# Rope by halves and probabilities split before their turn, in a four-layer kernel on one core

## The chip, the core and the metric

The kernel runs on one core of a Trainium2 chip. The metric is the device time of one execution in microseconds (us). The engines are TensorE (PE, with its weight loads PEld), VectorE (DVE), ScalarE (ACT), GpSimd (POOL) and SyncE (SP), which issues most of the transfers. Each runs its own list of instructions in the order in which the kernel writes them, and they wait for each other by semaphores.

## The reference, cut to what matters

Two layers, each of attention and a feed-forward part, over 16 batches of 128 tokens with 512 features. The change is in the first attention (and a little in the expert part behind it):

```python
x = x + xattn(layernorm(x), ctx)           # <- the change is in here
x = x + moe(layernorm(x))                  # 16 experts, 6 per token; its last blocks change order
x = x + memory_attention(layernorm(x), ctx)
x = x + peer_and_mlp(layernorm(x))

# xattn, 16 heads, per batch of 128 queries and 128 keys
kv_c, q_c = kv @ W_kvc, q @ W_dq
q_nope, q_rope = q_c @ W_uq, rope(q_c @ W_qr)      # rope on 64 columns per head
k_nope, v, k_rope = kv_c @ W_uk, kv_c @ W_uv, rope(kv_c @ W_kr)
scores = (q_nope . k_nope + q_rope . k_rope) * scale, masked by seg_id
out = softmax(scores) @ v @ W_o
# rope: concat(x1*cos - x2*sin, x1*sin + x2*cos)
```

The weights W_uk and W_uv are folded into the query and output weights ahead of this stage. Products are made of 16-bit pairs: a value is held as `hi` (rounded to 16 bits) and `lo` (what is left), and `mm3` issues three matmuls, hi by hi, hi by lo, lo by hi.

## The kernel before

The attention stage is a software pipeline of 64 **steps** (`STEPS`). Step m works on tile t = m // 4 (a batch of 128 tokens) and on head group g = m % 4 (four heads). In one step TensorE does, in this order: the scores of step m; the query product of the next tile's group (`heads_pe`) and, for g 0 and 1, the next tile's rope product in halves of eight heads (`rope_pe`); the turn of the probabilities of step m-2 (`turn_prob`); the value product of step m-3; the output product of step m-4. So each product's operands are made by the other engines in the steps between.

**The probabilities.** `exps(m)` on ScalarE writes exp(scores) into `prob`, in float32. VectorE takes the reciprocal of the sums at the start of its next step (`reciprocals`, L1560). GpSimd multiplies (`normalize`, L2092, in place). In step m+2 TensorE turns four 128x128 float32 squares into bank 2 (L887), ScalarE copies them as `pt_hi` (`prob_high`, L1250), VectorE writes `pt_lo` from the bank and `pt_hi` (`prob_low`, one `lo_of`, L1461), and `values` takes both in step m+3.

**The rope.** For the next tile, VectorE multiplies by cosine and sine in steps g=0 and g=1 (`rope_dve`, L1540, L1544). In step g=2 GpSimd adds the two products over all 16 heads (`rope_sum_pool`, L2084), ScalarE rounds the sum to 16 bits (`rope_act`, L1220) and GpSimd writes the rest (`rope_low_pool`, L2088). TensorE turns the first eight heads late in step g=3 (`rope_turn(t + 1, 0)`, L846), ScalarE copies them out right behind `exps` (`rope_copy`, L1224), and the scores of the next tile's first step (L871) wait for that copy.

**What else lies in these queues.** For finished tiles there is a chain of one tile in four steps: `row_rstd` (g=0); `row_normalize` on VectorE, `row_high` on ScalarE (L1261) behind `exps`, `row_low` on GpSimd (L2102), all g=1 from step 9; a turn and its copy `rows_turned` (g=2, L1277); `logits` (g=3). GpSimd issues batches of four scatters of token numbers (`place_batch`, L2106) at the end of three steps in eight from step 19. Two pieces of expert weights per step, in steps 0 to 55, are split into halves by ScalarE (`split_act`, L1289) and VectorE (`split_dve`, L1461 on SBUF operands). ScalarE's order in a step is: `heads_act` (L1231), `prob_high`, `values_high`, `exps` (L1237 and L1242), `row_high`, `rows_turned`, `rope_act`, `rope_copy`, `split_act`. VectorE's is: `reciprocals`, `maxima`, a split, `heads_dve`, `prob_low`, `values_low`, `rope_dve`, routing, a split.

The expert stage behind it runs 111 blocks (`NBLK`) through `expert_up`, `turn_rows`, `turn_hidden` and `expert_down`; each block's output goes out by an indirect add to `x_sum` (L2175), one after the other.

## Time and profile before

| what | us |
|---|---|
| median of 3 runs | 2100.8 |
| lowest and highest | 2089.52, 2101.47 |
| profiled execution, its own time | 2079.02 |
| its span, first to last instruction | 2077.2 |
| attention stage, first scores to the end of the routing | about 180 to 712 |
| expert stage | about 732 to 1450 |
| memory attention, then the last feed-forward part | to 2077 |

The profiled execution was faster than all three timed runs, so sums are made against 2079.0 and carried to the median as a difference. TensorE is busy 88% of the span, VectorE 59%, ScalarE 42% and GpSimd 39%. In a row of the timeline the first number is the start in us from the span's start, the second the duration; a bracket at the end says how long the engine stood idle before and what released it. "L2084" is a line of the kernel before; most lines name one operation, but L1461 is the helper `lo_of` and L205 to L207 are `mm3`.

### The profile page before, as it was taken

Reading aid. Unit: us, or ns where it says so; the run is one execution under the profiler, and the core shown is the slowest. Engines: PE = TensorE matmul, PEld = TensorE weight load, DVE = VectorE, ACT = ScalarE, POOL = GpSimd, SP = SyncE. Lnnn points to the kernel's source line nnn. Section 1 sums busy time; section 2 is a strip of 40 time slices with the busy share of each in tenths; the row PEclk is TensorE's granted clock in tenths of the full one; section 3 lists DMA queues with packets and bytes.
Section 4 is the critical chain, followed back from the end, with each engine's and each line's share of the span. In section 5 each row is a group of like instructions: output and inputs, shape, how many; then the busy total and the mean of one; then the engine's idle time right before and its main releaser. Section 6 shows DMA issues by size and latency. Waiting matters only on the chain.

```text
span 2077.2 us, 39689 instructions
## 1 busy us (share of the span) xinstructions
PE 1834.4 (88%) x13029; PEld 1085.9 (52%) x13029; DVE 1225.5 (59%) x2650; ACT 875.3 (42%) x1774; POOL 809.9 (39%) x659
## 2 busy tenths in 40 slices
PE   2575999989889389999999999996569989999998
PEld 1334666656656156666666666664434434444443
DVE  7854787877776333343333333331785677777776
ACT  3435777777776134344444444442232222212211
POOL 3102336554565533443344334432101334544542
PEclk6697999999999789999999999998789999999999
DMA  5313558667675266666666665544200346565554
GB/s 196 111 61 106 174 172 176 186 160 186 155 173 133 55 176 167 143 148 169 141 158 144 149 167 113 97 90 69 97 35 4 114 143 199 166 209 198 192 183 162
DMA packets 149136, 294.82 MB, mean 142 GB/s; under 512 B 40432, under 2 KB 77936, under 8 KB 144688
## 3 DMA queue, kind: packets, MB, share of 16 engines
q1 hardware_dynamic: 97968, 157.48, 26.4%
q0 software_dynamic: 46368, 126.29, 24.8%
q10 hardware_dynamic: 4608, 8.52, 1.3%
q8 instruction: 116, 1.90, 0.4%
q14 instruction: 76, 0.62, 0.1%
HBM read 426.00 MB, written 78.33 MB: 243 GB/s over the span
## 4 chain that ended last, share of the span: by engine, by line
PE 68%; DVE 10%; issue 6%; POOL 6%; ACT 5%; DMA 4%; SPq 0%; POOLq 0%; ACTq 0%; DVEq 0%
PE bank L205 19%; PE bank L206 19%; PE bank L207 19%; POOL expert_tokens L2106 3%; PE bank L999 2%; DVE work_arena L1461 2%; PE bank L1026 2%; DVE work_arena L168 1%; DVE ln_st L155 1%; ACT xt_arena L1242 1%; POOL work_arena L2088 1%; DMA work_arena<-in_moe_w 1%; POOL xt_arena L2092 1%; DMA work_arena<-in_ctxT 1%; DMA x_sum<-x,work_arena 1%
## 5 line engine op out<-in xcount | busy, mean ns | idle before, releaser
L205 PE MATMUL bank<-work_arena,xt_arena 128*128 (+1 forms) x1285 | 417.1, 327 | 0.9 <-ACT xt_arena L1370 0.9
L206 PE MATMUL bank<-work_arena,xt_arena 128*128 (+1 forms) x1285 | 416.9, 326 | 0.0
L207 PE MATMUL bank<-work_arena,xt_arena 128*128 (+1 forms) x1285 | 416.8, 326 | 0.0
L2175 POOL DMA_INDIRECT x_sum<-x,work_arena x111 | 175.5, 1581 | 400.0 <-ACT x L1389 201.9
L205 PE MATMUL bank<-work_arena 128*128 128x512 f16 (+1 forms) x680 | 261.8, 387 | 47.6 <-DVE work_arena L1461 18.8
L1934 DVE TENSOR_TENSOR xt_arena<-xt_arena,bank 128x352 f32<-128x352 f32 x111 | 57.8, 521 | 371.2 <-PE bank L207 371.2
L206 PE MATMUL bank<-work_arena 128*128 128x512 f16 (+1 forms) x680 | 261.7, 387 | 0.0
L207 PE MATMUL bank<-work_arena 128*128 128x512 f16 (+1 forms) x680 | 260.1, 384 | 0.0
L205 PE MATMUL bank<-xt_arena,work_arena 128*128 128x512 f16 (+1 forms) x560 | 212.7, 380 | 1.0 <-DVE xt_arena L174 1.0
L206 PE MATMUL bank<-xt_arena,work_arena 128*128 128x512 f16 (+1 forms) x560 | 212.5, 379 | 0.0
L207 PE MATMUL bank<-xt_arena,work_arena 128*128 128x512 f16 (+1 forms) x560 | 212.4, 379 | 0.0
L1370 ACT ACTIVATE xt_arena<-bank 128x1024 f16<-128x1024 f16 x111 | 113.7, 1024 | 222.1 <-PE bank L999 222.1
L2182 POOL TENSOR_TENSOR work_arena<-work_arena 128x512 f16<-128x512 f32 x64 | 73.6, 1170 | 270.5 <-ACT work_arena L1355 270.5
L1461 DVE SCALAR_TENSOR_TENSOR work_arena<-work_arena 128x1024 f16<-128x1024 f32 (+3 forms) x117 | 140.7, 1203 | 63.6 <-ACT work_arena L1289 55.7
L207 PEld LDWEIGHTS bank<-work_arena,xt_arena 128*128 128x128 f16 x1285 | 126.5, 98 | 85.3
L205 PEld LDWEIGHTS bank<-work_arena,xt_arena 128*128 128x128 f16 x1285 | 126.5, 98 | 80.6 <-issue 1.0
L206 PEld LDWEIGHTS bank<-work_arena,xt_arena 128*128 128x128 f16 x1285 | 126.5, 98 | 80.1 <-issue 0.3
L2191 POOL DMA_INDIRECT work_arena<-in_pk_e,work_arena x128 | 136.2, 1064 | 35.0 <-issue 31.3
L205 PEld LDWEIGHTS bank<-work_arena 128*128 128x128 f16 x680 | 69.7, 102 | 126.2 <-DVE work_arena L1461 24.5
L1461 DVE SCALAR_TENSOR_TENSOR work_arena<-bank,work_arena 128x512 f16<-128x512 f32 (+1 forms) x176 | 110.4, 659 | 31.6 <-ACT work_arena L1250 9.8
L2162 POOL DMA_INDIRECT x<-token_rows,work_arena x111 | 110.4, 995 | 44.4 <-issue 26.5
L1757 DVE SCALAR_TENSOR_TENSOR x<-bank,x 128x512 f32<-128x512 f32 x128 | 88.2, 691 | 60.3 <-PE bank L207 60.2
(255 smaller groups left out, 3793.4 us busy)
## 6 DMA issues: line engine op xcount, KB each, us to landing
work_arena<-expert_w SPq DMA_DIRECT2D x111, 1408.0 KB
work_arena<-expert_w SPq DMA_DIRECT2D x111, 768.0 KB
work_arena<-in_moe_w SPq DMA_DIRECT2D x64, 352.0 KB
expert_w<-work_arena SPq DMA_DIRECT2D x86, 176.0 KB
work_arena<-in_moe_w SPq DMA_DIRECT2D x48, 256.0 KB
work_arena<-in_mlp_w SPq DMA_DIRECT2D x8, 1536.0 KB, 9.6
work_arena<-in_head_w SPq DMA_DIRECT2D x16, 512.0 KB, 3.6
expert_w<-work_arena SPq DMA_DIRECT2D x64, 128.0 KB
```

Of the source, the lines that this page charges most:

```text
L205: pe.matmul(o, a_hi, b_hi, start=start, stop=False)
L206: pe.matmul(o, a_hi, b_lo, start=False, stop=False)
L207: return pe.matmul(o, a_lo, b_hi, start=False, stop=stop)
L1370: act.activation(xT[:, b % 2, :], bank[4][:, :].bitcast(F16), ACT.Copy).then_inc(xt_cp, 1)
L1461: return dve.scalar_tensor_tensor(out=o, in0=src, scalar=scale, in1=hi, op0=ALU.mult, op1=ALU.subtract)
L1757: dve.scalar_tensor_tensor(out=xv, in0=bank[6 + q % 2][:, :], scalar=1 / (WS * WS), in1=xv, op0=ALU.mult, op1=ALU.add).then_inc(xadd[q % 2 ...
L1934: dve.tensor_tensor(em[:, b % 2, :], esg[:, b % 2, :], bank[2 + b % 2][:, 0:MOE_D], ALU.mult).then_inc(e_m, 1)
L2106: pool.indirect_dma_start(out=recs[:, :], out_offset=bass.IndirectOffsetOnAxis(ap=ridx[:, t, k:k + 1], axis=0), in_=rtok[:, t:t + 1].bitca ...
L2162: pool.indirect_dma_start(out=xbu[:, b % XB, :], out_offset=None, in_=rows[:, :], in_offset=bass.IndirectOffsetOnAxis(ap=rid[:, i:i + 1], ...
L2175: pool.indirect_dma_start(out=xacc[:, :], out_offset=bass.IndirectOffsetOnAxis(ap=rid[:, i:i + 1], axis=0), in_=ysb[:, b % YB, :], in_offs ...
L2182: pool.tensor_tensor(h_lo[:, S_ % 2, c, :], m2[:, c, :], h_hi[:, S_ % 2, c, :], ALU.subtract).then_inc(hlo, 1)
L2191: pool.indirect_dma_start(out=gbuf[:, n % 2 * SETS + i - FIRST[n], :], out_offset=None, in_=ins["pk_e"][:, :], in_offset=bass.IndirectOffs ...
```

## The change

Three things are done.

1. **Rope by halves.** `rope_sum_pool`, `rope_act` and `rope_low_pool` work on eight heads at a time (a = 0, 1), twice as many instructions of half the size. The first half's sum and rounding move to step g=1, its rest to g=2; the second half follows one step behind. `rope_turn(t + 1, 0)` moves ahead in step g=3, to right behind the query product.
2. **Probabilities split first.** `normalize` writes its product as 16 bits into a new buffer `prob16`. `prob_low` now reads SBUF alone (`prob` in float32 and `prob16`), in four instructions of 128x128 that scale by the reciprocal, and runs one step earlier (m-1 in place of m-2), behind GpSimd's `normalize` of the same step. `turn_prob` turns eight 16-bit squares. `prob_copy` takes them out in one copy of 128x1024, in place of `prob_high` and the old `prob_low`. `prob` has two buffers in place of three. The factor 64 on the probabilities is gone.
3. **The last expert blocks** are put in another order on TensorE, so that each turn of the hidden values stands behind an `expert_down`.

The gate weights' buffers move to another place in memory.

```diff
             def turn_prob(m):
-                pe.wait_ge(normed, m + 1)
-                need(pe, ptl, m)
-                for i in range(4):
-                    last = pe.transpose(bank[2][:, i * P:(i + 1) * P], prob[:, m % 3, i, :], id32[:, :])
+                pe.wait_ge(plow, m + 1)
+                need(pe, pt_cp, m)
+                o = bank[2][:, :].bitcast(F16)
+                for i in range(8):
+                    last = pe.transpose(o[:, i * P:(i + 1) * P], prob16[:, m % 2, i * P:(i + 1) * P], id16[:, :])
                 last.then_inc(pt_mm, 1)
...
                     if g < 2:
                         rope_pe(t + 1, g)
+                    if g == 3:
+                        rope_turn(t + 1, 0)
...
-                if g == 3 and t + 1 < NT:
-                    rope_turn(t + 1, 0)
...
-            for b in range(NBLK):
-                if b + 1 < NBLK:
-                    expert_up(b + 1, slots[b + 1])
-                if b + 2 < NBLK:
-                    slots[b + 2] = slot_of(b + 2)
-                    turn_rows(b + 2)
+            for b in range(NBLK - 2):
+                expert_up(b + 1, slots[b + 1])
+                slots[b + 2] = slot_of(b + 2)
+                turn_rows(b + 2)
                 turn_hidden(b)
                 if b > 0:
                     expert_down(b - 1, slots.pop(b - 1))
-            expert_down(NBLK - 1, slots.pop(NBLK - 1))
+            expert_down(NBLK - 3, slots[NBLK - 3])
+            turn_hidden(NBLK - 2)
+            expert_up(NBLK - 1, slots[NBLK - 1])
+            expert_down(NBLK - 2, slots[NBLK - 2])
+            turn_hidden(NBLK - 1)
+            expert_down(NBLK - 1, slots[NBLK - 1])
...
-            def rope_act(t):
-                act.wait_ge(rope_sum, t + 1)
+            def rope_act(t, a):
+                hs = slice(8 * a, 8 * a + 8)
+                act.wait_ge(rope_sum, 2 * t + a + 1)
                 if t > 0:
-                    act.wait_ge(tr_mm, tr_at["turn", t - 1, 1] + 1)
-                act.activation(rhl[:, :, 0, :], rot, ACT.Copy).then_inc(rope_h, 1)
+                    act.wait_ge(tr_mm, tr_at["turn", t - 1, a] + 1)
+                act.activation(rhl[:, hs, 0, :], rot[:, hs, :], ACT.Copy).then_inc(rope_h, 1)
...
-            def prob_high(m):
+            def prob_copy(m):
                 act.wait_ge(pt_mm, m + 1)
                 need(act, o_mm, m - 1)
-                act.activation(pt_hi[:, m % 2, :], bank[2][:, :], ACT.Copy, scale=PS).then_inc(pth, 1)
+                act.activation(pt[:, m % 2, :], bank[2][:, :].bitcast(F16), ACT.Copy).then_inc(pt_cp, 1)
...
                 if t + 1 < NT:
-                    if g == 2:
-                        rope_act(t + 1)
+                    if g in (1, 2):
+                        rope_act(t + 1, g - 1)
...
             def prob_low(m):
-                dve.wait_ge(pth, m + 1)
-                lo_of(pt_lo[:, m % 2, :], bank[2][:, :], PS, pt_hi[:, m % 2, :]).then_inc(ptl, 1)
+                dve.wait_ge(normed, m + 1)
+                for i in range(4):
+                    last = dve.scalar_tensor_tensor(out=prob16[:, m % 2, (4 + i) * P:(5 + i) * P],
+                                                    in0=prob[:, m % 2, i, :], scalar=rinv[:, m % 4, i:i + 1],
+                                                    in1=prob16[:, m % 2, i * P:(i + 1) * P], op0=ALU.mult,
+                                                    op1=ALU.subtract)
+                last.then_inc(plow, 1)
...
-                if m >= 2:
-                    prob_low(m - 2)
+                if m >= 1:
+                    prob_low(m - 1)
...
-            def rope_sum_pool(t):
-                pool.wait_ge(q_free, q_at["rope", t, 1] + 1)
-                pool.tensor_tensor(rot, rt1, rt2, ALU.add).then_inc(rope_sum, 1)
-
-            def rope_low_pool(t):
-                pool.wait_ge(rope_h, t + 1)
-                pool.tensor_tensor(rhl[:, :, 1, :], rot, rhl[:, :, 0, :], ALU.subtract).then_inc(rope_l, 1)
+            def rope_sum_pool(t, a):
+                hs = slice(8 * a, 8 * a + 8)
+                pool.wait_ge(q_free, q_at["rope", t, a] + 1)
+                pool.tensor_tensor(rot[:, hs, :], rt1[:, hs, :], rt2[:, hs, :], ALU.add).then_inc(rope_sum, 1)
+
+            def rope_low_pool(t, a):
+                hs = slice(8 * a, 8 * a + 8)
+                pool.wait_ge(rope_h, 2 * t + a + 1)
+                pool.tensor_tensor(rhl[:, hs, 1, :], rot[:, hs, :], rhl[:, hs, 0, :], ALU.subtract).then_inc(rope_l, 1)
...
-                if t + 1 < NT and g == 2:
-                    rope_sum_pool(t + 1)
-                    rope_low_pool(t + 1)
+                if t + 1 < NT:
+                    if g in (1, 2):
+                        rope_sum_pool(t + 1, g - 1)
+                    if g in (2, 3):
+                        rope_low_pool(t + 1, g - 2)
```

The new order on GpSimd, in steps 9 and 10 (tile 2, g=1 and g=2). Before (L2092 `normalize`, L2102 `row_low`, L2084 `rope_sum_pool`, L2088 `rope_low_pool`):

```order
L2092 TENSOR_TENSOR xt_arena<-xt_arena,work_arena 128x512 [waits recip]
L2102 TENSOR_TENSOR xt_arena<-xt_arena 128x512 [waits row_hi]
L2092 TENSOR_TENSOR xt_arena<-xt_arena,work_arena 128x512 [waits recip]
L2084 TENSOR_TENSOR work_arena<-work_arena 128x1024 [waits q_free]
L2088 TENSOR_TENSOR work_arena<-work_arena 128x16x64 [waits rope_h]
```

and now (L2107 `normalize`, L2117 `row_low`, L2097 the sum of a half, L2102 the rest of a half):

```order
L2107 TENSOR_TENSOR xt_arena<-xt_arena,work_arena 128x512 [waits pt_mm,recip]
L2117 TENSOR_TENSOR xt_arena<-xt_arena 128x512 [waits row_hi]
L2097 TENSOR_TENSOR work_arena<-work_arena 128x512 [waits q_free]
L2107 TENSOR_TENSOR xt_arena<-xt_arena,work_arena 128x512 [waits pt_mm,recip]
L2097 TENSOR_TENSOR work_arena<-work_arena 128x512 [waits q_free]
L2102 TENSOR_TENSOR work_arena<-work_arena 128x8x64 [waits rope_h]
```

The first half's sum now stands behind `row_low`, which waits for ScalarE's `row_high` of the same step.

ScalarE in the same tile, from `exps` of step 9 to the copies of step 10. Before (L1242 `exps`, L1261 `row_high`, L1265 the store of x, L1289 splits, L1231, L1250 and L1255 the copies of step g=2):

```order
L1242 ACTIVATE xt_arena,work_arena<-bank,work_arena 128x128 x3
L1261 ACTIVATE xt_arena<-xt_arena 128x512 [waits t_norm]
L1265 DMA x_sum<-x 128x512 [waits yadd]
L1289 ACTIVATE work_arena<-work_arena 128x512 [waits split_out0,split_in0]
L1289 ACTIVATE xt_arena<-work_arena 128x512 [waits split_out1,split_in1]
L1231 ACTIVATE xt_arena<-bank 128x512 [waits score_mm,q_mm]
L1250 ACTIVATE work_arena<-bank 128x512 [waits o_mm,pt_mm]
L1255 ACTIVATE work_arena<-bank 128x512 [waits y_mm,o_mm]
```

and now (L1267 `row_high`, L1226 `rope_act` of the first half, L1295 splits, L1256 `prob_copy`):

```order
L1248 ACTIVATE xt_arena,work_arena<-bank,work_arena 128x128 x3
L1267 ACTIVATE xt_arena<-xt_arena 128x512 [waits t_norm]
L1271 DMA x_sum<-x 128x512 [waits yadd]
L1226 ACTIVATE work_arena<-work_arena 128x8x64 [waits tr_mm,rope_sum]
L1295 ACTIVATE work_arena<-work_arena 128x512 [waits split_out0,split_in0]
L1295 ACTIVATE xt_arena<-work_arena 128x512 [waits split_out1,split_in1]
L1237 ACTIVATE xt_arena<-bank 128x512 [waits score_mm,q_mm]
L1256 ACTIVATE work_arena<-bank 128x1024 [waits o_mm,pt_mm]
L1261 ACTIVATE work_arena<-bank 128x512 [waits y_mm,o_mm]
```

`rope_act` of the first half has come in between `row_high` and the splits, with its wait for GpSimd's sum.

## Rows read from the trace of the kernel before

**Rows 1.** Stretches: us, busy of PE, PEld, DVE, ACT, POOL, granted clock, DMA.

```profile
420.00:660.00 240.00, 217.65 (x2088) 144.81 (x2088) 186.99 (x388) 177.83 (x453) 126.32 (x102) 0.96 0.64 164
357.60:361.00 3.40, 3.36 (x14) 1.74 (x15) 3.40 (x6) 3.15 (x11) 1.04 (x1) 0.50 0.47 96
```

**Rows 2.** Waits from 180 to 700 us: who waited for whom, us in total, times, longest.

```profile
PE bank L846 <- POOL work_arena L2088: 20.7, 14, 3.7
...
PE bank L871 <- ACT work_arena L1224: 14.6, 10, 3.3
```

**Rows 3.** ScalarE in order of time, steps 13 to 15: start us, us, engine, line.

```profile
279.06 0.60 ACT L1250 ACTIVATE work_arena<-bank 128x512 f16<-128x512 f32 x1 [0.92 <-PE bank L887]
...
282.28 0.63 ACT L1261 ACTIVATE xt_arena<-xt_arena 128x512 f16<-128x512 f32 x1
282.80 1.15 ACT L1289 ACTIVATE work_arena<-work_arena 128x512 f16<-128x512 f32 x2
284.74 0.60 ACT L1231 ACTIVATE xt_arena<-bank 128x512 f16<-128x512 f32 x1 [0.80 <-PE bank L860]
...
289.76 1.07 ACT L1220 ACTIVATE work_arena<-work_arena 128x1024 f16<-128x1024 f32 x1
...
294.49 0.30 ACT L1237 ACTIVATE work_arena<-work_arena 128x4 f32<-128x4 f32 x1 [0.84 <-DVE work_arena L1555]
...
296.57 1.03 ACT L1224 ACTIVATE work_arena<-bank 128x1024 f16<-128x1024 f16 x1
```

**Rows 4.** GpSimd in order of time, steps 13 and 14.

```profile
282.99 1.16 POOL L2102 TENSOR_TENSOR xt_arena<-xt_arena 128x512 f16<-128x512 f32 x1 [4.99 <-ACT xt_arena L1261]
284.86 1.04 POOL L2092 TENSOR_TENSOR xt_arena<-xt_arena,work_arena 128x512 f32<-128x512 f32 x1 [0.72 <-DVE work_arena L1560]
285.86 2.79 POOL L2084 TENSOR_TENSOR work_arena<-work_arena 128x1024 f32<-128x1024 f32 x1
290.90 2.13 POOL L2088 TENSOR_TENSOR work_arena<-work_arena 128x1024 f16<-128x1024 f32 x1 [2.25 <-ACT work_arena L1220]
```

**Rows 5.** VectorE in order of time, steps 13 to 16.

```profile
278.20 0.68 DVE L1461 SCALAR_TENSOR_TENSOR xt_arena<-work_arena,xt_arena 128x512 f16<-128x512 f32 x1
...
286.37 0.68 DVE L1461 SCALAR_TENSOR_TENSOR xt_arena<-bank,xt_arena 128x512 f16<-128x512 f32 x1
...
291.54 2.25 DVE L1461 SCALAR_TENSOR_TENSOR xt_arena<-work_arena,xt_arena 128x704 f16<-128x704 f32 x1 [3.29 <-ACT xt_arena L1289]
...
298.31 0.89 DVE L1461 SCALAR_TENSOR_TENSOR work_arena<-work_arena 128x704 f16<-128x704 f32 x1 [0.24 <-ACT work_arena L1289]
```

**Rows 6.** TensorE in order of time, step 15 and the start of step 16.

```profile
293.09 0.62 PE L846 MATMUL bank<-id,work_arena 128*128 128x128 f16 x8 [0.39 <-POOL work_arena L2088]
...
297.65 0.39 PE L871 MATMUL bank<-work_arena,idbf 128*128 128x512 bf16 x1 [1.35 <-ACT work_arena L1224]
```

**Rows 7.** TensorE's turns, 180 to 700 us: busy us, mean ns | idle before.

```profile
L887 PE MATMUL bank<-id,xt_arena 128*128 128x128 f32 x256 | 39.2, 276 | 3.1 <-POOL xt_arena L2092 1.8 <-DVE work_arena L1461 1.1
...
L846 PE MATMUL bank<-id,work_arena 128*128 128x128 f16 x248 | 21.7, 238 | 20.7 <-POOL work_arena L2088 20.7
```

**Rows 8.** GpSimd's groups by shape, same stretch and columns.

```profile
L2106 POOL DMA_INDIRECT expert_tokens<-work_arena x85 | 90.6, 1066 | 25.6 <-issue 22.7 <-DVE work_arena L1649 2.9
```

**Rows 9.** GpSimd, steps 45 and 46.

```profile
542.13 1.16 POOL L2102 TENSOR_TENSOR xt_arena<-xt_arena 128x512 f16<-128x512 f32 x1 [4.48 <-ACT xt_arena L1261]
...
549.70 2.36 POOL L2084 TENSOR_TENSOR work_arena<-work_arena 128x1024 f32<-128x1024 f32 x1
```

**Rows 10.** ScalarE, step 46.

```profile
552.09 1.06 ACT L1220 ACTIVATE work_arena<-work_arena 128x1024 f16<-128x1024 f32 x1 [3.07 <-POOL work_arena L2084]
```

**Rows 11.** TensorE, step 47.

```profile
555.40 0.91 PE L846 MATMUL bank<-id,work_arena 128*128 128x128 f16 x8 [3.55 <-POOL work_arena L2088]
```

**Rows 12.** GpSimd at the end of the expert stage.

```profile
1434.36 1.54 POOL L2175 DMA_INDIRECT x_sum<-x,work_arena  x1 [4.32 <-ACT x L1389]
1439.76 1.54 POOL L2175 DMA_INDIRECT x_sum<-x,work_arena  x1 [3.86 <-DMA x_sum<-x,work_arena]
```

63 lines of the change are left out of this document (34 added, 29 removed).

## The prediction

> **What bounds the kernel now.** I read the page's busy shares first, then busy time by stretch, then the waits of the attention stage, and last the timeline of one tile on each engine. TensorE bounds nearly everything: between 420 and 660 us it is busy 217.7 of 240 us, with ScalarE at 177.8 and VectorE at 187.0 [rows 1]. What is left to win in this stage are TensorE's waits, and two carry them: the turn of the rope (L846) waits 20.7 us for GpSimd, and the scores behind it (L871) wait 14.6 us for ScalarE's copy of that turn [rows 2]. Both fall once per tile, around the border from g=3 to g=0. A long one costs more: after the 3.55 us of idleness in step 47 [rows 11] the turn took 0.91 us in place of 0.62 [rows 6]. In another such place the granted clock was 0.50 for 3.40 us, the lower of the two levels (1.2 GHz in place of 2.4) [rows 1]; that loses up to 3.40/2 = 1.7 us of work. So the two waits and some five such pieces are worth 20.7 + 14.6 + 5 x 1.7 = 44 us at most.
>
> There are two kinds of border. **Free** ones, where no scatters are queued: 0.39 us at the turn and 1.35 us at the scores [rows 6], at tiles 3, 4, 5, 7, 9, 11 and 13 (seven). **Scatter** ones, where four scatters of 1.07 us with 0.3 us between them (5.3 us) [rows 8] hold up GpSimd's sum: about 3.5 us at the turn [rows 11], at tiles 6, 8, 10, 12 and 14 (five). Tiles 1 and 2 come before the rows' chain begins, and tile 15 after the weight splits end.
>
> **What sets a free border.** The example is the border at 297.65 us, into tile 4. ScalarE ends `exps` of step 13 and does `row_high` at 282.28, the splits at 282.80, stands idle 0.80 us for TensorE; it rounds the rope sum at 289.76, is idle 0.84 us for VectorE's maxima at 294.49, and makes the copy at 296.57 [rows 3]. So of the 13.8 us from 282.80 to 296.57 it stands idle some 1.6 us and works the rest. That slack is what the change has to live in.
>
> **Part 1, the rope by halves.** TensorE's wait at the turn goes where it came from the 2.13 us of `rope_low_pool` at 290.90 [rows 4]: the first half's rest is now made in step g=2. But the turn isn't the last link; the scores need the copy, and that stays behind `exps` on ScalarE. And ScalarE gets a new wait. Its order in step g=1 is now `exps`, `row_high`, `rope_act` of the first half, splits. That `rope_act` waits for GpSimd's first sum, and on GpSimd that sum stands behind `row_low`, which waits for this very `row_high`. The chain: `row_high` starts at 282.28; `row_low` started 0.71 us later, at 282.99, and took 1.16 [rows 3, 4]; the half sum takes half of the 2.36 us that L2084 takes alone, 1.2 us; some 0.1 us to be seen. 282.28 + 0.71 + 1.16 + 1.2 + 0.1 = 285.45 us, against 282.80 when ScalarE is free: **a new wait of 2.6 us**, in steps 9, 13, ... 57, thirteen of them. Queued behind it are the splits (and VectorE's split and next reciprocal, which wait for them), the query copy, `prob_copy`, `values_high` and `exps` of step 14. The halving adds 0.1 us on ScalarE (two instructions of some 0.55 us for one of 1.07).
>
> (The 2.36 us is the sum at 549.70 us [rows 9], where VectorE was quiet; the one at 285.86 took 2.79 [rows 4] with the end of a VectorE split beside it.)
>
> **Part 2, probabilities split first.** On TensorE eight 16-bit squares replace four float32 ones: 39.2 us in 64 turns is 0.61 us each, and the 16-bit turns of eight squares took 21.7 us in 31, 0.70 us, some of them at the lower clock [rows 7]. At 293.09, at the full clock, such a turn took 0.62 us [rows 6]. I take 0; the ends are -1 and +6 us over 64 steps (0.09 each). The Trainium skill ("FP8 and Floating Point Precision", TensorE Precision Notes) says that a true float32 product takes four passes through the array, by which the old turn would be double the new one; the row shows no such thing here, and it decides.
>
> On ScalarE a copy of 128x1024 16-bit values from PSUM takes 1.02 us (L1224), the old `prob_high` 0.60 us (L1250) [rows 3]: **+0.42 us per step**, two to three of them between the anchor of step 13 and the copy at the border.
>
> On VectorE four instructions of 128x128 replace one from PSUM. The split of 512 columns takes 0.68 us, of 704 columns 0.89 us [rows 5], so 1.1 ns per column, and one of 128 columns 0.68 - 384 x 0.0011 = 0.26 us; four are 1.05 us, or 0.9 with the overlap of neighbours, against 0.68: +0.3 us per step. VectorE stood idle 3.29 us ahead of its split in step 14 [rows 5], so this is hidden. It now waits for GpSimd's `normalize` of the same step. In the example that is done at 284.86 + 1.04 = 285.90, and VectorE comes to that place, behind the query's rest, at 286.37 + 0.68 = 287.05 [rows 4, 5]: 1.15 us to spare, and as much or more in nearly all steps, also with a 16-bit output that costs 0.1 us more (`row_low`, 1.16). Where scatters stand ahead of it, VectorE will wait 0.5 to 4 us (steps 21, 22, 30, 38, 46, 54, and the last five). Those in g=2 are the scatter borders.
>
> A collision belongs here. VectorE's split of 704 columns took 2.25 us at 291.54, where `rope_low_pool` ran until 293.03, and 0.89 us at 298.31 [rows 4, 5]: 293.03 - 291.54 = 1.49 us of waiting, then its usual time. The two exclude each other. The new `prob_low` has both operands in SBUF, and the halves of the rope run on GpSimd just then in g=2. Worst case it loses both halves, 2.3 us. The Trainium skill ("SBUF — State Buffer", Who interferes with whom) says that a VectorE instruction with two SBUF inputs fully blocks against a GpSimd one that reads SBUF, whichever starts first; the trace agrees, and this speaks against reading the probabilities from SBUF while GpSimd is busy. In return the 1.49 us at 291.54 go, since the halves lie elsewhere.
>
> **The free border worked out.** ScalarE from its new release at 285.45, which I round up to 285.8 since `prob_copy` of step 13 already came 0.42 us late: `rope_act` 0.5, splits 1.1, query copy 0.5, `prob_copy` 1.0, `values_high` 0.5, `exps` 2.1, `rows_turned` 0.9, `rope_act` 0.5, splits 1.35, query copy 0.5, `prob_copy` 1.0, `values_high` 0.55, `exps` 2.05, the copy 1.0: 13.6 us without a gap, by the start to start times of [rows 3]. The scores start at 299.3 us in place of 297.65: **+1.65 us**. VectorE would have had the maxima ready at 295.3, 0.9 us before ScalarE asks, so ScalarE is the bound. TensorE's 0.39 us at the turn turns into a wait for the first half's rest of about 1.2 us, and the one at the scores grows from 1.35 to some 2.3 us. Seven borders: +11.5 us.
>
> **The scatter border.** Its chain is GpSimd's: `row_low` at 542.13 [rows 9], four scatters, `normalize`, the sum, for which ScalarE waited 3.07 us until 552.09 [rows 10]. Now a half sum stands ahead of the scatters and half behind `normalize`, so the second `rope_act` starts at 552.7. `prob_low` on VectorE waits for the late `normalize`, and TensorE's turn now stands ahead of `turn_prob` and the values, which are held up with it. By ScalarE's 0.6 us the next scores come 0.5 us later; by TensorE's held-up work (0.45 us of turn and 0.65 of values, double that at the lower clock) up to 2.2 us. I take +1, nearer to ScalarE's row, since the copy and not TensorE was last at the free borders. Five: +5 us.
>
> **The rest.** Filling: the first two borders have no `row_low` in the way. The first turn follows half a rounding and half a `rope_low_pool` earlier (0.5 + 1.06 = 1.5 us), and the next border half a rounding and the 1.49 us of collision (2 us): -3.5. Tile 15: no splits any more, -0.4. Draining: GpSimd is the bound there; the last `prob_low` stands ahead of `row_normalize(14)` and waits for the last `normalize`: +1.5. Clock: more idleness at the free borders may bring pieces at half clock that weren't there; I take one, +1.7, and leave seven (+12) as the upper bound. The last expert blocks: the adds to `x_sum` go one after the other, 1439.76 - 1434.36 = 5.4 us apart [rows 12], and only the first of them can come earlier, since it waited for ScalarE's row: -0.5. Moving the gate weights: 0.
>
> **Sum.** 11.5 + 5 - 3.5 - 0.4 + 1.5 + 1.7 - 0.5 = +15.3 us, 2094.3 against the profiled 2079.0, and 2116.1 against the median of 2100.8. The profiled execution lay 21.8 us under the median, so the three runs themselves spread by 0.6%; I take 1% (21 us) as what a measurement here can tell from no change.
>
> **Rivals.**
> 1. *The waits just go.* If ScalarE's new wait falls into slack that I don't see, for instance because the pipeline runs a step deeper ahead of TensorE, the waits at the free borders go (7 x 1.74 = 12 us), those at the scatter borders shrink by the 2.1 us by which the first half's rest is ready earlier (5 x 2.1 = 10 us), with two or three pieces at half clock (4 us), and the filling (3.5): -28 us or so, 2073. For it: TensorE's turn is the wait that the chain of waits names, and 20.7 us of it is real. Against it: ScalarE has 1.6 us of slack where 2.6 + 2 x 0.42 are added. Chance 0.18.
> 2. *Slower than the sum.* Every free border loses its 1.7 us of clock (+10 beyond the sum), the scatter borders cost 2.2 us (+6), and `prob_low` blocks against the halves (+0.5 us in some of 13 tiles, +5): 2100.8 + 15 + 21 = 2137. It decides once TensorE's idleness at a free border, 0.4 + 1.35 = 1.7 us before, comes near the 3.55 us of [rows 11], behind which the clock was low. Chance 0.32, which takes in the upper part of the sum's own spread.
> 3. *The change does nothing here.* Off the critical path by compensation: -3.5 and the free borders at 0 instead of +1.65, if `row_low`'s start is earlier than I have it. 2100. It belongs to the forecast's own range. Forecast with this: 0.50.
>
> **How the numbers follow.** The forecast's own range is 2096 to 2126; with the rivals the range is 2080 to 2138. Faster by over 1%: rival 1 at its better half and more, 0.16. Slower by over 1% (above 2122): rival 2 and a small part of the forecast, 0.36. Within 1%: 0.48.
>
> **What would show it.** In the trace of the changed kernel: ScalarE's L1226 waits about 2.4 us for GpSimd's L2097 in thirteen tiles, some 31 us together. The scores' wait for the copy (L1230) grows from 14.6 us to 20 or more, in spite of the earlier turn. VectorE's new `prob_low` takes 0.9 to 1.1 us per step, longer in g=2. The copies L1256 take 1.02 us. From one tile's first scores to the next it takes 1 to 2 us more. I am wrong if L1226 shows no wait, or if it shows one and the scores' spacing doesn't grow (then ScalarE has more slack than [rows 3] says).

## The result and the profile after

The changed kernel takes 2107.57 us (median of 14 runs, 2101.03 to 2114.65), the kernel before beside it on the same chip 2099.32 us (14 runs, 2089.52 to 2106.79): a ratio of **1.0045, interval 1.0033 to 1.0058**, which is 0.0045 x 2100.8 = 9.5 us more where 15.3 were forecast. Within 1%, as forecast. On a second chip the same kernel stood at 1.0082 (1.0051 to 1.0113, its median 2101.67 us), so the loss has been seen between 9 and 17 us (0.0082 x 2100.8). One execution of e5 below took 4974.74 us and is left out of its ratio.

The profiled executions took 2079.02 us before and 2110.11 after. The first lay 20 us under its median, the second 3 above, so the 31 us between the two traces overstate the change; what counts is where they lie. Where in the kernel before its other executions lose those 20 us isn't known, and every comparison with its one profile below carries that. TensorE's first work on the gathered rows of the expert stage starts at 756.0 us in place of 732.2. So 24 of the 31 us lie in the attention stage and its draining; from there to the last add the changed kernel needs 5 us more (1 of them between the last adds), and the rest is 2 us longer. The 5 us behind the attention stage stand in the profile of the second chip too; the kernels e3 and e5 with the same expert stage need 1 us more, so no cause is named for them.

The stretches answer to [rows 1] (us, busy of PE, PEld, DVE, ACT, POOL, granted clock, DMA share, GB/s). The second is the stretch in which TensorE was busy for 217.7; the last line is the kernel before in the first stretch:

```profile
180.00:420.00 240.00, 214.00 (x2196) 147.84 (x2196) 194.23 (x419) 185.73 (x456) 105.04 (x88) 0.95 0.61 163
420.00:660.00 240.00, 213.49 (x2131) 144.18 (x2132) 195.60 (x454) 179.69 (x436) 127.94 (x112) 0.94 0.66 160
...
180.00:420.00 240.00, 218.25 (x2171) 151.10 (x2171) 182.40 (x338) 182.30 (x464) 108.26 (x81) 0.96 0.65 172
```

TensorE's busy time fell by 4.2 us in each stretch, VectorE's grew by 8.6 in the second and 11.8 in the first. Who waited for whom from 180 to 700 us, to be held against [rows 2]:

```profile
ACT work_arena L1226 <- POOL work_arena L2097: 32.0, 17, 2.5
ACT work_arena L1256 <- PE bank L889: 27.9, 33, 2.7
...
DVE xt_arena L1573 <- POOL xt_arena L2107: 22.1, 7, 7.0
...
PE bank L872 <- ACT work_arena L1230: 20.8, 12, 3.7
...
PE bank L847 <- POOL work_arena L2102: 18.2, 6, 3.7
```

ScalarE's new wait for the half sum is there, 32.0 us. The scores' wait for ScalarE's copy (L872) grew from 14.6 to 20.8 us, and the turn's wait for GpSimd (L847) fell only from 20.7 to 18.2. The two kinds of border differ here: at the seven free ones the turn waited 0.39 us each for GpSimd and waits for it no more, while the six waits that are left are those at the five scatter borders (2.1 to 3.7 us, together 15.0; before, 1.6 to 3.7 and 14.7) and at the first border. The border that answers to the worked example, into tile 4, on ScalarE in order of time [rows 3]:

```profile
284.80 0.63 ACT L1267 ACTIVATE xt_arena<-xt_arena 128x512 f16<-128x512 f32 x1
287.92 0.63 ACT L1226 ACTIVATE work_arena<-work_arena 128x512 f16<-128x512 f32 x1 [2.49 <-POOL work_arena L2097]
288.45 1.13 ACT L1295 ACTIVATE work_arena<-work_arena 128x512 f16<-128x512 f32 x2
289.49 0.58 ACT L1237 ACTIVATE xt_arena<-bank 128x512 f16<-128x512 f32 x1
289.97 1.01 ACT L1256 ACTIVATE work_arena<-bank 128x1024 f16<-128x1024 f16 x1
...
294.35 0.64 ACT L1226 ACTIVATE work_arena<-work_arena 128x512 f16<-128x512 f32 x1
...
296.71 1.04 ACT L1256 ACTIVATE work_arena<-bank 128x1024 f16<-128x1024 f16 x1
...
300.21 1.03 ACT L1230 ACTIVATE work_arena<-bank 128x1024 f16<-128x1024 f16 x1
```

and on GpSimd [rows 4]:

```profile
285.50 1.16 POOL L2117 TENSOR_TENSOR xt_arena<-xt_arena 128x512 f16<-128x512 f32 x1 [5.00 <-ACT xt_arena L1267]
286.62 1.27 POOL L2097 TENSOR_TENSOR work_arena<-work_arena 128x512 f32<-128x512 f32 x1
289.96 1.04 POOL L2107 TENSOR_TENSOR xt_arena<-xt_arena,work_arena 128x512 f16<-128x512 f32 x1 [2.07 <-DVE work_arena L1568]
290.95 1.72 POOL L2097 TENSOR_TENSOR work_arena<-work_arena 128x512 f32<-128x512 f32 x1
292.63 1.21 POOL L2102 TENSOR_TENSOR work_arena<-work_arena 128x512 f16<-128x512 f32 x1
```

From `row_high` at 284.80 by `row_low` and the half sum to `rope_act` at 287.92 it is 3.12 us; the working had 3.17. After it ScalarE has no gap until the copy at 300.21. TensorE stands idle twice there, against 0.39 and 1.35 us in [rows 6]. The turn now waits for ScalarE's copy of the turned rows (L1283), which uses the same bank, and no more for GpSimd, whose rest of the first half was done at 293.84:

```profile
294.62 0.61 PE L847 MATMUL bank<-id,work_arena 128*128 128x128 f16 x8 [1.08 <-ACT xt_arena L1283]
...
301.29 0.39 PE L872 MATMUL bank<-work_arena,idbf 128*128 128x512 bf16 x1 [2.08 <-ACT work_arena L1230]
...
566.86 1.03 PE L847 MATMUL bank<-id,work_arena 128*128 128x128 f16 x8 [3.29 <-POOL work_arena L2102]
...
573.79 0.39 PE L872 MATMUL bank<-work_arena,idbf 128*128 128x512 bf16 x1 [1.10 <-ACT work_arena L1230]
```

The lower two are a scatter border: the turn still waits 3.29 us, where it was 3.55 in [rows 11], and takes 1.03 us: from 566.8 to 568 us, behind that idleness, the granted clock was 0.50. On VectorE the low half runs from SBUF while GpSimd does the second sum and the first half's rest; the line above it is a step in which GpSimd has nothing to do:

```profile
281.91 1.12 DVE L1573 SCALAR_TENSOR_TENSOR xt_arena<-xt_arena,work_arena 128x128 f16<-128x128 f32 x4
...
292.07 2.44 DVE L1573 SCALAR_TENSOR_TENSOR xt_arena<-xt_arena,work_arena 128x128 f16<-128x128 f32 x4
```

The times from a tile's first scores to the next tile's, read from the starts of L871 (L872) and summed over the seven free borders (into tiles 3, 4, 5, 7, 9, 11, 13) and the five scatter borders (6, 8, 10, 12, 14), are the yardstick for all kernels below. There is one profile of each, so a few us are no finding. "Stalls" are idle times of TensorE inside the scatter tiles that the trace puts down to "issue", more of which in the last section; where there are pieces of over 1 us, the value in brackets is without these. The changed kernel's first profile has 2.9 us of shorter pieces in its scatter tiles, and without them it comes to the 178.7 of the second chip; e2 has 1.3 us.

| kernel | first two tiles | 7 free | 5 scatter | into tile 15 |
|---|---|---|---|---|
| before | 56.6 | 218.2 | 170.0 | 29.2 |
| changed | 57.2 | 223.1 | 181.5 | 30.5 |
| changed, second chip | 57.0 | 223.1 | 178.7 | 30.5 |
| e1 rope alone | 56.8 | 215.6 | 173.1 | 29.7 |
| e2 probabilities alone | 58.1 | 221.5 | 174.1 | 29.5 |
| e3 sum first | 56.9 | 228.0 | 169.5 | 30.3 |
| e5 sum and copy first | 53.0 | 222.5 | 173.4 | 29.9 |
| f2 low half last | 57.0 | 230.3 | 177.8 | 34.5 |
| f3 low half in one, wrong data | 56.7 | 229.5 | 200.4 | 30.5 |
| f4 high half taken twice | 57.0 | 218.4 | 190.4 | 29.7 |
| g3 low half zero, in one | 57.0 | 223.5 | 188.6 (181.8) | 30.5 |
| g4 copy of the high half | 56.9 | 218.8 | 180.3 (174.2) | 29.7 |
| g34 both | 59.0 | 217.2 | 187.4 (178.7) | 29.7 |
| f1 old probabilities, sum and copy first | 52.0 | 217.7 | 178.7 (167.8) | 29.8 |

### The profile page after: what moved, and what is told of

The parts are those of the page before. It is cut to its first block, busy times and chain, and to the rows that moved or that the text cites. A ratio compares the mean times of both kernels' runs of the same rounds, so it can differ in the third digit from the quotient of the medians.

```text
span 2108.3 us, 40515 instructions
## 1 busy us (share of the span) xinstructions
PE 1852.2 (88%) x13281; PEld 1096.3 (52%) x13285; DVE 1259.4 (60%) x2842; ACT 896.8 (43%) x1790; POOL 823.6 (39%) x691
## 4 chain that ended last, share of the span: by engine, by line
PE 62%; issue 11%; DVE 9%; POOL 7%; ACT 5%; DMA 4%; another core or an unknown queue 0%; SPq 0%; ACTq 0%; POOLq 0%; DVEq 0%
PE bank L202 18%; PE bank L204 18%; PE bank L203 18%; DMA x_sum<-x,work_arena 3%; POOL expert_tokens L2121 3%; PE bank L1001 2%; DVE work_arena L1468 2%; PE bank L1028 2%; POOL xt_arena L2107 1%; DVE work_arena L165 1%; POOL work_arena L2097 1%; DVE ln_st L152 1%; ACT xt_arena L1248 1%; POOL xt_arena L2117 1%; POOL work_arena L2102 1%
## 5 line engine op out<-in xcount | busy, mean ns | idle before, releaser
L202 PE MATMUL bank<-work_arena,xt_arena 128*128 (+2 forms) x1349 | 425.3, 320 | 8.0 <-DVE xt_arena L171 3.3
L203 PE MATMUL bank<-work_arena,xt_arena 128*128 (+2 forms) x1349 | 424.7, 320 | 0.0
L204 PE MATMUL bank<-work_arena,xt_arena 128*128 (+2 forms) x1349 | 424.6, 320 | 0.0
L1377 ACT ACTIVATE xt_arena<-bank 128x1024 f16<-128x1024 f16 x111 | 113.7, 1024 | 224.7 <-PE bank L1001 188.5
L202 PEld LDWEIGHTS bank<-work_arena,xt_arena 128*128 128x128 f16 x1349 | 132.8, 99 | 85.3 <-issue 4.5
L204 PEld LDWEIGHTS bank<-work_arena,xt_arena 128*128 128x128 f16 x1349 | 132.2, 99 | 85.5 <-issue 0.6
L203 PEld LDWEIGHTS bank<-work_arena,xt_arena 128*128 128x128 f16 x1349 | 132.5, 99 | 80.5 <-issue 0.8
L1468 DVE SCALAR_TENSOR_TENSOR work_arena<-work_arena 128x704 f16<-128x704 f32 (+2 forms) x118 | 127.0, 1077 | 48.8 <-ACT work_arena L1295 24.1
L2107 POOL TENSOR_TENSOR xt_arena<-xt_arena,work_arena 128x512 f16<-128x512 f32 x64 | 67.0, 1046 | 165.0 <-DVE work_arena L1568 159.3
```

Source lines behind the costliest of these rows:

```text
L202: pe.matmul(o, a_hi, b_hi, start=start, stop=False)
L203: pe.matmul(o, a_hi, b_lo, start=False, stop=False)
L204: return pe.matmul(o, a_lo, b_hi, start=False, stop=stop)
L1377: act.activation(xT[:, b % 2, :], bank[4][:, :].bitcast(F16), ACT.Copy).then_inc(xt_cp, 1)
L1468: return dve.scalar_tensor_tensor(out=o, in0=src, scalar=scale, in1=hi, op0=ALU.mult, op1=ALU.subtract)
L2107: pool.tensor_tensor(prob16[:, m % 2, 0:4 * P].rearrange("p (a b) -> p a b", a=4), prob[:, m % 2, :, :], rinv[:, m % 4, :].unsqueeze(2).to ...
```

## The experiments

Three groups, each on one chip with the kernel before beside it (medians of that kernel: 2081.36, 2084.48 and 2096.63 us). Ratios are to that kernel. Since the changed kernel itself stood at 1.0045 and at 1.0082 on two chips, ratios of different groups are compared only where they differ by more.

**The two parts alone.** The kernel before with the rope's part of the diff (halves and the earlier turn), and the kernel before with the probabilities' part. The second also has the gate weights' buffers at their new place; neither has the new order of the last expert blocks.

> The kernel before with the rope by halves and the earlier turn alone; probabilities and the last expert blocks as before. Theory A (ScalarE's new wait for GpSimd's first half sum, behind row_low, is what the change pays for): the wait of 2.5 us shows up in 13 tiles (some 30 us in all), and eats what the earlier turn gives: -5 to +5 us against before. Theory B (the probabilities' path is what costs, the rope by halves is a gain): 15 to 25 us faster than before.

> The kernel before with the probabilities split first alone; rope and expert blocks as before. Theory A: ScalarE has the slack for 0.42 us per step as long as it doesn't also wait for the half sum; what is left is VectorE's wait behind the scatters and a longer drain: +3 to +10 us against before. Theory B: +20 us or more.

Rope alone: 2078.73 us, **0.9978** (0.9960 to 0.9996). Probabilities alone: 2093.63 us, **1.0060** (1.0037 to 1.0084), +12 us. Their product is 1.0038, near the whole's 1.0045: the loss comes with the probabilities' part. The -2.6 us of the rope lie in the -5 to +5 expected of theory A; the +12 us of the probabilities lie between the two theories' ranges, nearer to A's +3 to +10. With the rope alone ScalarE waits as long for the half sum as in the whole:

```profile
ACT work_arena L1221 <- POOL work_arena L2088: 37.5, 19, 2.5
PE bank L871 <- ACT work_arena L1225: 19.7, 14, 3.7
PE bank L846 <- POOL work_arena L2093: 18.2, 6, 3.6
```

and yet the seven free tiles are 2.6 us shorter than before. So the rope's part as a whole, with this wait in it, costs nothing there. What the wait costs within it, against what the earlier turn gives, this run doesn't separate; that it costs only in company with the longer copies is argued, not shown. With the probabilities alone the waits of TensorE behind the new order show:

```profile
DVE xt_arena L1567 <- POOL xt_arena L2099: 23.3, 9, 4.8
PE bank L889 <- DVE xt_arena L1567: 15.4, 8, 4.0
PE bank L872 <- ACT work_arena L1226: 15.0, 12, 3.3
```

The 15.4 us at the turn of the probabilities (L889) are 0.2 and 3.3 us in the two profiles of the whole. So a part of what e2 loses is lost at another place than in the whole, and the product of the two ratios doesn't say that the same waits add up.

**The wait for the sum taken away, then the copy brought forward.** In e3, GpSimd's half sum stands ahead of `row_low` in step g=1, so that ScalarE finds it done. In e5, ScalarE's copy of the first half's turn also stands ahead of the exponentials at g=3.

```diff
+                if t + 1 < NT and g in (1, 2):
+                    rope_sum_pool(t + 1, g - 1)
                 if row_tile(m, 1) is not None:
                     row_low(row_tile(m, 1))
...
+                if t + 1 < NT and g == 3:
+                    rope_copy(t + 1, 0)
                 exps(m)
```

> The changed kernel with GpSimd's half sum ahead of row_low in step g=1. Theory A: ScalarE's wait of 32 us for the sum falls to under 8 us, the scores' wait for the copy (20.8 us) to under 8 us, seven free borders get 3.3 us shorter each: 15 to 25 us faster than the changed kernel, 5 to 15 us faster than before. Theory B: within 5 us of the changed kernel, since the prob_copy and the SBUF-only split still bound it.

> The same with ScalarE's copy of the first turned half (step g=3) put ahead of exps. Theory A: the scores' wait for the copy vanishes at all borders (under 2 us in all) and the five scatter borders gain some 2 us each as well: 15 to 30 us faster than before. Theory B: no faster than e3_sum_first.

e3: 2092.41 us, **1.0048** (1.0026 to 1.0070). e5: 2085.19 us, **1.0011** (0.9990 to 1.0032). The forecast of 15 to 25 us faster than the changed kernel fell for e3, and that of 15 to 30 us faster than the kernel before for e5. The waits of e3 in 180 to 700 us:

```profile
PE bank L872 <- ACT work_arena L1230: 19.5, 12, 3.7
...
PE bank L847 <- POOL work_arena L2102: 12.5, 5, 3.2
PE bank L932 <- DVE xt_arena L1468: 10.8, 5, 2.4
...
ACT work_arena L1226 <- POOL work_arena L2097: 3.0, 5, 1.8
```

The wait for the sum is down from 32.0 to 3.0 us, and at the borders into tiles 3 and 4 the period is 29.9 us where the changed kernel has 31.7 and 31.8: there the wait was worth 1.8 us, near the 1.65 us that the working of the free border has. But from tile 5 on, where the router's ranks (L932) run, free tiles take 32.3 to 34.2 us: TensorE's wait for VectorE ahead of the ranks doubles from 5.5 to 10.8 us, and what was won comes back. In e5 that wait is 17.7 us, and the scores' wait for the copy 7.6; the first two tiles are 4 us shorter than in the changed kernel, the only kernels with that gain being those with the copy brought forward.

**Which engine's time does the probabilities' path cost?** The control is the changed kernel again.

> The changed kernel unchanged, so that the three edits beside it have it on the same chip. Every theory expects about 1.0045 of the kernel before.

2101.67 us, **1.0082** (1.0051 to 1.0113).

f2 moves VectorE's `prob_low(m - 1)` from the step's start to its end, ahead of the last split.

> The changed kernel, but VectorE makes the probabilities' low half (the four instructions of L1573) at the end of its step, ahead of the split of the same step, and not at the step's start. Theory V1 (VectorE is held up because it waits there for GpSimd's normalize, 22.1 us in the changed kernel, with the rope's work and the maxima queued behind it): the wait at L1573 goes, and 5 to 12 us of the 9 with it. Theory V2 (what costs is VectorE's time in the four instructions, 1.57 us per step, wherever they stand): no gain. If the later low half holds up TensorE's turn of the probabilities instead, TensorE's wait at L889 for L1573 grows from 5 us to 15 or more and the kernel gets slower by 5 us.

2106.54 us, **1.0097** (1.0065 to 1.0129): no gain. VectorE's wait for `normalize` fell from 21.3 us in the control to 9.3, the ranks' wait grew to 11.5 and the scores' to 26.1. TensorE's wait at L889 stayed at 3.6 us, so it isn't what kept the time up. What VectorE's wait itself costs isn't separated, since the later place brought these other waits.

f3 makes the low half in one instruction and leaves out the product with the reciprocal in it; f4 copies the high half alone, and the value product takes it twice:

```diff
-                for i in range(4):
-                    last = dve.scalar_tensor_tensor(... prob[:, m % 2, i, :], scalar=rinv[:, m % 4, i:i + 1], ...)
+                last = lo_of(prob16[:, m % 2, 4 * P:8 * P], prob[:, m % 2, :, :]..., 1.0, prob16[:, m % 2, 0:4 * P])
...
-                act.activation(pt[:, m % 2, :], bank[2][:, :].bitcast(F16), ACT.Copy).then_inc(pt_cp, 1)
+                act.activation(pt[:, m % 2, 0:4 * P], bank[2][:, :].bitcast(F16)[:, 0:4 * P], ACT.Copy).then_inc(pt_cp, 1)
```

> The changed kernel, but the low half of the probabilities is made in one VectorE instruction of 128x512 in place of four of 128x128; it leaves out the product with the reciprocal in the low half. One such instruction from SBUF I estimate at 0.7 us by the split of 512 columns in the kernel before, so it takes 0.8 to 0.9 us per step off VectorE, 55 us in 64 steps. Theory V2 (VectorE's time is what costs): 5 to 12 us faster than the changed kernel, so 0.99 to 1.00 of the kernel before. Theory V1 (the place of the wait): under 3 us. Theory S (ScalarE's copy, 0.42 us longer): nothing.

> The changed kernel, but ScalarE copies the high half of the turned probabilities alone (512 of 1024 16-bit columns), and the values' product takes the high half twice. The copy should go from 1.02 us to 0.6, as the old one from float32 took. Theory S (ScalarE is the bound at the free borders, so its 0.42 us per step, some two of them per border, are part of the loss): 7 to 12 us faster than the changed kernel. Theory V2: no difference, since VectorE comes last.

f3: 2127.64 us, **1.0191** (1.0157 to 1.0225). f4: 2101.81 us, **1.0075** (1.0048 to 1.0102), no different from the control. Both misses. ScalarE's weight splits wait long for their loads in both; of f3 and of f4:

```profile
ACT work_arena L1295 <- DMA work_arena<-in_moe_w: 30.4, 15, 7.2
...
ACT xt_arena L1295 <- DMA work_arena<-in_moe_w: 10.7, 5, 4.5
```

```profile
ACT work_arena L1295 <- DMA work_arena<-in_moe_w: 33.6, 13, 5.5
...
ACT xt_arena L1295 <- DMA work_arena<-in_moe_w: 11.5, 6, 3.3
```

These are 41 and 45 us in all, against 12.0 + 3.1 = 15 us in the control; only e5 has as much (41 us), and it isn't slow, so this wait alone doesn't explain them. In both kernels the edit changes the attention's output much, and so what the router does with the tokens. Even so f4's free tiles are short, 218.4 us against 223.1; its scatter tiles are long. So the two edits were made again with data near the right ones: g3 multiplies by zero in one instruction of the same shape and operands, and g4 copies all 1024 columns in the first two steps and the high half alone after that.

```diff
+                last = dve.scalar_tensor_tensor(out=prob16[:, m % 2, 4 * P:8 * P], in0=prob[:, m % 2, :, :]...,
+                                                scalar=0.0, in1=prob16[:, m % 2, 0:4 * P],
+                                                op0=ALU.mult, op1=ALU.mult)
...
+                w = slice(0, 8 * P if m < 2 else 4 * P)
+                act.activation(pt[:, m % 2, w], bank[2][:, :].bitcast(F16)[:, w], ACT.Copy).then_inc(pt_cp, 1)
```

> The changed kernel with the probabilities' low half set to zero by one VectorE instruction of 128x512 with the same operands in place of four of 128x128; it leaves out the low half of the probabilities and nothing else, so that the routing of the tokens stays nearly that of the changed kernel. If the 20 us by which the earlier form of this edit was slower came from its other data (the router's scatters and expert blocks), this one is not slower than the changed kernel; if VectorE's 0.8 us per step is what the changed kernel loses, it is 5 to 10 us faster. If it is slower again, with ScalarE's weight splits waiting some 40 us for their loads, then the DMA traffic of the splits that falls out of step is the cause, and not the data.

> The changed kernel, but from the third step on ScalarE copies the turned probabilities' high half alone (128x512 in place of 128x1024), so the values' product takes the low halves of the first two steps over again; it leaves out the later low halves. The free borders should take 30.8 us per tile in place of 31.7, as in the form of this edit that took the high half twice. If that one's long scatter borders (up to 41.5 us) came from its data, this is 5 to 8 us faster than the changed kernel; if they come from the transfers' timing, it is no faster.

> Both edits at once: one VectorE instruction that sets the low half to zero, and ScalarE's copy of the high half alone; it leaves out the low half of the probabilities. It brings VectorE and ScalarE back to about their times before, on the changed kernel's order. If the engines' times explain the loss, it comes to 0.997 to 1.000 of the kernel before, as the rope by halves alone did; if the order (TensorE's turn of the probabilities behind GpSimd and VectorE) costs by itself, it stays at 1.004 or above.

g3: 2113.02 us, **1.0081** (1.0062 to 1.0100). g4: 2097.17 us, **0.9997** (0.9983 to 1.0011). g34: 2103.94 us, **1.0037** (1.0024 to 1.0051). The waits for the loads are gone from g3 (6 us) and g4 (12 us). What differs from f3 and f4 is the data and the chip; that the data did it is the likelier reading, not a shown one.

g4 is the finding. Its copies from 180 to 700 us (busy us, mean ns | idle before):

```profile
L1257 ACT ACTIVATE work_arena<-bank 128x512 f16<-128x512 f16 x62 | 36.9, 596 | 35.2 <-PE bank L889 21.3 <-remote 13.7
```

596 ns each where the changed kernel's take 1024. With that edit the changed kernel stands at the time of the kernel before: 0.5 to 0.8% below its own ratios on the other two chips. It wasn't run on this chip, so the cleanest measure of the copy is g34 against g3, which differ by the copy alone and ran side by side: 0.44% less, with intervals that don't touch. 62 x 0.43 = 27 us of ScalarE's time are gone in g4, and 4.3 us at the free borders with some 4 to 7 at the scatter borders came out of it in the table (the last with the stalls left out). So the longer copy is shown to cost, 0.4% at least. That it is the whole loss isn't shown: f4, the same shorter copy with wrong data, stood at 1.0075 beside the control's 1.0082.

g3 shows the other side. Its low half, all 64 (ns min/median/max):

```profile
L1572 DVE SCALAR_TENSOR_TENSOR xt_arena<-xt_arena x64: 672/693/2845, 191.8 to 713.1; 128x512 f16<-128x512 f32 x64
```

The mean is 1.01 us against 1.57 for the four instructions, so VectorE has 0.56 us per step more, and nothing comes of it: 1.0081 stands inside what the changed kernel showed, and the seven free tiles take 223.5 us against 223.1. The same edit on top of g4, which is g34, even comes out 0.4% slower, with intervals that don't touch. So no gain from VectorE's time is seen in either pair. Why g34 is slower than g4 stays open; its longer part in the table is the scatter tiles, in one profile. With it a rival stays open that g34 was made to tell: its 1.0037 (1.0024 to 1.0051) lies just under the 1.004 that was named for a cost of the new order by itself, and well above the 0.997 to 1.000 that the engines' times alone would give, while g4, with the same order, shows no such cost.

**The version made of what was learnt.** f1 is the kernel before with the rope by halves, the half sum ahead of `row_low` and the copy ahead of the exponentials; the probabilities as before.

> The kernel before with the rope by halves, GpSimd's half sum ahead of row_low in step g=1, and ScalarE's copy of the first half's turn ahead of the exponentials at the border; the probabilities' path stays as before. The two free borders' waits are then taken on (ScalarE's wait for the sum, 32 us in the changed kernel, and the scores' wait for the copy, 20 us), and VectorE has its old load. If the borders are what bounds and VectorE has slack with the old path, this is 10 to 20 us faster than the kernel before (0.990 to 0.995). If VectorE comes last even so (as it did with the new path: the ranks waited 17.7 us for its split), it is within 5 us of the rope by halves alone, 0.998.

2078.37 us against 2096.63, **0.9917** (0.9891 to 0.9943): 17 us faster than the kernel before, and by its ratio the fastest of all. Its order is that of e5 (1.0011) with the old probabilities, another 0.9% between them, on different chips; the changed kernel's own ratio moved by 0.4% between two chips. The first two tiles take 52.0 us, tiles 3 and 4 28.3 each, where the kernel before had 30.2 and 30.4 in the table's count. The ranks are late in it too:

```profile
DVE work_arena L1463 <- ACT work_arena L1290: 52.6, 25, 5.3
...
PE bank L930 <- DVE xt_arena L1463: 16.0, 6, 3.3
PE bank L846 <- POOL work_arena L2093: 10.1, 5, 2.8
...
ACT work_arena L1221 <- POOL work_arena L2088: 8.7, 6, 2.5
```

The 16.0 us ahead of the ranks are the largest of TensorE's waits that are left there.

Not tried: the old order of the last expert blocks in the changed kernel, since its 1 us can't be told by a measurement of this one.

## Why the prediction was right, and where it was not

The time was right (+15.3 us forecast, +9.5 measured, up to +17 on the second chip), and so were the sign and the class. The terms under it were not all: the free borders came out 6.6 us under their term and the scatter borders 6.5 us over theirs, and that these two nearly cancel was luck. The terms below are read against the one profile of the kernel before, which was 20 us faster than its median, so a few us of each are open.

**ScalarE's new wait: right.** 31 us in thirteen tiles were forecast, and 13 x 2.49 = 32.4 came, where 2.6 or 2.4 each were named. (The 32.0 us above are eleven of these and six shorter ones, mostly for the second half's sum; the two others are the 5.0 us that the trace puts down to "issue".) The chain from `row_high` took 3.12 us against 3.17. That it costs at the free borders is shown by e3 for tiles 3 and 4 (1.8 us each, against +1.65 in the working). With the rope alone (e1) the same wait left no loss; whether because it costs nothing without the longer copies, or because the earlier turn pays for it, no run separates. TensorE's wait of about 1.2 us at the turn came in size (1.08 us at tiles 3 and 4), but behind ScalarE's L1283 and not behind the first half's rest.

**The free borders: too high.** +11.5 us were forecast; the seven took 223.1 - 218.2 = 4.9 us more. The step that failed is "Seven borders": +1.65 was worked out for the border into tile 4, where +1.4 came (31.8 against 30.4, and +1.5 at tile 3), and was carried to five others, where the old period was already 31.3 to 31.7 us and 0 to +0.8 came. Those five have the router's ranks in them (L930 at 310.8, 375.6, 443.2, 508.1 and 573.2 us in the trace before); one example stood for two kinds.

**The scatter borders: too low.** +5 were forecast with +1 each, +11.5 came (2.3 each), 8.7 without the stalls and 8.7 in the profile of the second chip (1.7 each). The upper end of the step, "up to 2.2 us" by TensorE's held-up work, was nearer in size, though no run shows that it is this held-up work; the lower was taken "since the copy and not TensorE was last at the free borders". e1 and e2 show that each part brings some of it (+3.1 and +4.1).

**Filling: wrong.** -3.5 forecast, +0.6 measured. The step let the scores follow the turn; but the scores wait for ScalarE's copy, behind the exponentials: only e5 and f1, which bring the copy forward, have the gain (53.0 and 52.0 against 56.6).

**`prob_copy`: right in size, too small in weight.** 1.02 us forecast, 1.024 measured. It entered the sum only as part of the free border, while without the 0.43 us per step the time fell by 0.44% (g34 against g3) or by 0.5 to 0.8% (g4 against the changed kernel on other chips), and g4 gains at the scatter borders too.

**VectorE's `prob_low`: right, with more collisions than foreseen.** 0.9 to 1.1 us per step were forecast, longer in g=2; the mean is 1.57. The price of the four instructions was nearly right: 0.26 us from one's start to the next's, as worked out, and 1.12 to 1.14 us for the four in the 31 steps in which no arithmetic of GpSimd ran beside them. In g=2 they took 2.2 to 3.2 us, as foreseen. Not foreseen were the 1.42 us in 14 of the 16 steps g=3, where the second half's rest (L2102) runs beside them. That this is hidden held: g3 takes a third of VectorE's time for it away and gains nothing. The Trainium skill ("SBUF — State Buffer", Who interferes with whom) has a VectorE instruction with two SBUF inputs and a GpSimd one that reads SBUF shut each other out; the 2.44 us at 292.07, in which GpSimd ran until 293.84, agree, against the 1.12 us at 281.91.

**TensorE's turns: right.** Eight 16-bit squares take 39.9 us in 62 steps, 0.64 each, four float32 ones took 39.2 in 64, 0.61 each [rows 7]. The four passes that the Trainium skill ("FP8 and Floating Point Precision", TensorE Precision Notes) has for a float32 product would have made the old turn double the new one, and these times disagree for the turns.

**The rest.** Tile 15: -0.4 forecast, +1.3. Draining: +1.5 forecast; from tile 15's first scores to TensorE's first work on the gathered rows 82.9 us against 77.7, and 79.4 on the second chip, which is near the forecast. Clock: one piece (+1.7) was taken; the trace has some 17 us more at half clock from 180 to 700 us (9 us on the second chip), of which half is lost: 8.5 and 4.6 us, more than the term and within the upper bound of +12. These us are a part of the border times above, not beside them. The expert tail: -0.5 forecast, +1 in this profile: the adds of [rows 12] are 6.85 us apart at one place where the kernel before had 5.85, behind ScalarE's row:

```profile
1456.69 1.54 POOL L2194 DMA_INDIRECT x_sum<-x,work_arena  x1 [4.74 <-ACT x L1396]
1463.54 1.54 POOL L2194 DMA_INDIRECT x_sum<-x,work_arena  x1 [5.31 <-ACT x L1396]
```

**The rivals.** Rival 1 (the waits just go) did not come about: 20.8 + 18.2 us are left of them. The turn's waits at the free borders did go, and those of the scores grew. In f1, with the copy and the sum moved too and the old probabilities, 1.6 + 10.1 us are left. Rival 2 (2137) was nearer at the scatter borders and in the clock, but its free borders did not come.

## What to carry to other kernels

An engine that is only 75% busy can still be the one whose microseconds count: at a border where its work has no gap, 0.43 us per step on one instruction was worth 0.4% of the kernel or more, while 0.56 us per step on a busier engine gained nothing. Price an edit on the engine that is last at the handover, not by busy shares, and work out one example for each kind of tile before multiplying. Making an operand ready earlier gains nothing while its consumer's other input, here a copy queued behind the exponentials, comes last; move that first.

## What the runs showed of the hardware that was not expected

TensorE can stand idle for nothing that the trace shows. In all four profiles of the third group it did so for 8.0 to 16.2 us between 180 and 730 us, in the middle of runs of equal products, as here in g3:

```profile
343.53 0.22 PE L861 MATMUL bank<-work_arena 128*128 128x128 f16 x1
344.94 0.22 PE L857 MATMUL bank<-work_arena 128*128 128x128 f16 x1 [1.19 <-issue]
347.05 0.22 PE L858 MATMUL bank<-work_arena 128*128 128x128 f16 x1 [1.89 <-issue]
347.10 0.22 PE L859 MATMUL bank<-work_arena 128*128 128x128 f16 x1
```

In the ten others such idleness comes to 4.4 us in one (the changed kernel's first profile) and at most 1.3 in the rest. "issue" seems also to stand for a wait whose release the trace lacks: of the 4.4 us, 1.6 lie ahead of the scores of the border into tile 9, where the second chip's profile has the same 1.56 us as a wait for ScalarE's copy. The 1.2 and 1.1 us ahead of L872 in g4 and g34 look like this too; the ones in the middle of equal products don't. On the third chip the kernel before was 12 to 15 us slower than on the chips of the first two groups. Whether the stalls make that chip slower is open: the kernel before has no profile there, and the first measurement's chip was as slow (2099.32 us) with 0 and 4.4 us of them in its two profiles.

One VectorE instruction of 128x512 from SBUF took 0.69 us at the median and 2.85 at the longest (g3); four of 128x128, the same number of columns, took 1.12 us together at the least: small pieces cost per instruction. In the 33 steps in which arithmetic of GpSimd ran beside them the four took 1.99 us on average, in the 31 others 1.13.
